# GpSimd's list per sequence in another order: the row scatter moved to the next step, the recurrence's double product moved ahead of a root

## The chip, the core and the metric

The program runs on one core of a Trainium2 chip. A core has five engines that run side by side, each through its own list in order: TensorE (PE; its weight loads are PEld), VectorE (DVE), ScalarE (ACT), GpSimd (POOL) and SyncE (SP), which here only issues DMAs. They meet through semaphores. The metric is device microseconds (us) of one execution, from three executions of each kernel.

## The reference, cut to what is computed

```python
# x, ctx: (32 sequences, 256 tokens, 256 channels), float32
x = ln(x + attn(x))          # attn: a complex decaying recurrence along the sequence axis
x = ln(x + xattn(x, ctx))    # 16 heads, 256x256 scores per head and sequence, softmax
x = ln(x + ffn(x))           # every token goes to one of 8 experts (nearest centroid)

# recurrence, written as a step over the 32 sequences: state = c * state + x[n]
# xattn: out = softmax(q k') v + q; out = ln_g * norm(out) + ln_b
# ffn: xn = rms_norm(x); id = argmin |xn - centroid|^2; h = xn @ up_w[id];
#      y = (a * silu(g)) @ down_w[id]; out = y + x
```

## The kernel before, in words

The kernel has two phases. Phase one walks over the 32 sequences ("items"), one per step `t`, software-pipelined: in step `t` TensorE makes the scores of item `t` and the transposed scores of `t-1`, the projections of item `n = t+1`, the output of item `a = t-2` and the expert choice of item `b = t-3`. At the end of its way each of an item's 256 rows (a token with its norm and its number) is written to its expert's bucket in DRAM, at a row number ("slot") worked out on the chip. Phase two takes tiles of 128 rows out of the buckets and runs the experts' matrices over them; the change does not touch it.

Each engine has a `step(t)` of its own, written out by hand; within it the order is fixed. VectorE's step is a chain of 16 row maxima of the scores (L1243, one per head `h`), with the other work put between the heads: at `h == 0` the normalised rows of item b (`row`, L1258, waits for `rstd2`, GpSimd's root for the second layer norm); at 3 `u = (state + 1) * x` (L1266); at 5 to 8 division, adding the queries (`oq`, L1370, twice) and the expert choice (`pick`, ending in `onehot`, L1405); at 9 the statistics `mvx` of the attention's norm; at 11 `gain` twice (L1377) with the small `place` (L1418) between; at 12 `slot` (L1425) and `y2` twice (L1324); at 13 and 14 the statistics of the second norm (`mv`, L1233, called mv2 below).

GpSimd's step, in order: `conv_products` of item t+3 (`by_re`, L694, one product of 128x1024 that serves both parts of the recurrence), `weigh(b)` (`xw`, L752), the bias added to x1 (L782), `cut` of the queries (`q_lo`, L770), `offset(b)` (L761), `conv_real` (L702), the root `rstd1` (L727, L729), `conv_imag` first half (L710), `cut` of the keys (`k_lo`, L770), `conv_imag` second half (L713), the root `rstdx` of the attention's norm (L727, L729), the scatter of item b (L802: two indirect DMAs of 128 rows, after a wait for VectorE's `slot`), `conv_input` (L720), the root `rstd2`, and the four small operations of `rms` (L738 to L744).

Around it: SyncE writes `k_lo` to DRAM when the cut is done and reads it back stacked (`k_st`), and the next step's scores on TensorE (L1004) wait for that. ScalarE squares `xw` for the expert choice (L927), which `offset` waits for. The `row` buffer and `slot` are double. Behind the last sequence `lower` (L1352) on VectorE prepares the experts' weights, a subtraction of 128x2048 each.

Of the kernel before, what the change touches and what calls it, by code (L numbers as in the profile page):

```python
# [15 lines left out]
SEQ, TOK, C = 32, 256, 256  # L16
NCH = C // P
NTC = TOK // P
# [9 lines left out]
PAD = E * CAP  # L28
# [4 lines left out]
SLOT = 6  # L33
# [48 lines left out]
def build(nc, x, ctx_in, lmlg, theta, last_conv, Wq, bq, Wk, bk, Wv, bv, ln_g, ln_b, ffn_scale, centroids, up_w, down_w, out):  # L82
    stack = ExitStack()
    with stack:
# [16 lines left out]
        buckets = nc.dram_tensor("buckets", (PAD + P, ROWW), F32)  # L101
# [19 lines left out]
        def sb1(name, shape, dt=F32):  # L121
            return phase1.enter_context(nc.sbuf_tensor(name, shape, dt))
# [69 lines left out]
        row = sb1("row", [P, 2, NTC, ROWW])  # L192
# [9 lines left out]
        slot = sb1("slot", [P, 2, NTC], U32)  # L202
# [25 lines left out]
        neg_in, scat = [s["neg_in0"], s["neg_in1"]], [s["scat0"], s["scat1"]]  # L228

        def wait(eng, name, item, per=1, j=None):  # L230

            if not item.runtime and item.k >= SEQ:
                item, j = Item(0, SEQ - 1), per
            wait_value(eng, name, item.times(per, per if j is None else j))

        def wait_value(eng, name, v):

            sm = s[name] if isinstance(name, str) else name
            if isinstance(v, int):
                if v > 0:  # L240
                    eng.wait_ge(sm, v)
            else:
                eng.wait_ge(sm, v)
                after_register_wait(eng)

        def wait_ring(eng, sm, item, ring, per):

            if not item.runtime:
                while item.k >= SEQ:
                    item = item - ring  # L250
            wait_value(eng, sm, item.uses(ring) * per)
# [6 lines left out]
        def steps(eng, body):  # L258

            for n in range(-2, SEQ + 3):  # L260
                body(Item(0, n))

        def active(item):
            return item.within(0, SEQ)
# [271 lines left out]
        with nc.Block() as block:  # L536
# [114 lines left out]
            def _(pool):  # L651
                g = nc.gpsimd
# [34 lines left out]
                def conv_products(item):  # L687

                    if not active(item):
                        return  # L690
                    wait(pool, "conv", item - 1, 5)
                    if item.k == 1:
                        wait(pool, "x1_ok", item - 1, 2)
                    g.tensor_tensor(by_re[:, :, :, :], state[:, 0].unsqueeze(1).to_broadcast(both), pair_b, ALU.mult).then_inc(s["conv"], 1)  # L694

                def conv_real(item):

                    if not active(item):
                        return
                    wait(pool, "conv", item, 5, 1)  # L700
                    wait(pool, "u_ok", item - 1)
                    g.tensor_tensor(state[:, 0], by_re[:, 1], state[:, 1], ALU.subtract).then_inc(s["conv"], 1)  # L702
# [12 lines left out]
                def conv_input(item):  # L715
                    if not active(item):
                        return
                    wait_ring(pool, x_in[item.mod(2)], item, 2, 16)
                    wait(pool, "conv", item, 5, 4)
                    g.tensor_tensor(state[:, 0], state[:, 0], xt[:, item.mod(2)], ALU.add).then_inc(s["conv"], 1)  # L720

                def rstd(item, ready, per, mv, rs, done):

                    if not active(item):
                        return
                    wait(pool, ready, item, per)
                    g.tensor_scalar(rs[:, 0], mv[:, :, 1], LN_EPS, None, ALU.add).then_inc(s[done], 1)  # L727
                    wait(pool, done, item, 2, 1)
                    g.tensor_tensor(rs[:, 1], rs[:, 0], neg_half[:, :].to_broadcast([P, NTC]), ALU.pow).then_inc(s[done], 1)  # L729

                def rms(item):

                    if not active(item):
                        return
                    p = item.mod(2)
                    wait(pool, "rstd2", item, 2)
                    wait_ring(pool, scat[p], item - 2, 2, 16 * NTC)
                    g.tensor_tensor(ms2[:, 0], mv2[:, :, 1], rs2[:, 1], ALU.mult).then_inc(s["rms"], 1)  # L738
                    wait(pool, "rms", item, 4, 1)
                    g.tensor_tensor(ms2[:, 1], ms2[:, 0], rs2[:, 1], ALU.mult).then_inc(s["rms"], 1)  # L740
                    wait(pool, "rms", item, 4, 2)
                    g.tensor_scalar(ms2[:, 2], ms2[:, 1], RMS_EPS, None, ALU.add).then_inc(s["rms"], 1)
                    wait(pool, "rms", item, 4, 3)
                    g.tensor_tensor(row[:, p, :, C], ms2[:, 2], neg_half[:, :].to_broadcast([P, NTC]), ALU.pow).then_inc(s["rms"], 1)  # L744

                def weigh(item):

                    if not active(item):
                        return
                    wait(pool, "x2_ok", item, 2)  # L750
                    wait(pool, "nx_ok", item - 1, 2)
                    g.tensor_tensor(xw[:, :, :], row[:, item.mod(2), :, 0:C], scale_bc[:, :].unsqueeze(1).to_broadcast([P, NTC, C]),  # L752
                                    ALU.mult).then_inc(s["xw_ok"], 1)

                def offset(item):

                    if not active(item):
                        return
                    wait(pool, "nx_ok", item, 2)
                    wait(pool, "pick", item - 1, PICK, 2)  # L760
                    g.tensor_tensor(dist[:, 0], cent_norm[:, :].unsqueeze(1).to_broadcast([P, NTC, E]),  # L761
                                    nx[:, :].unsqueeze(2).to_broadcast([P, NTC, E]), ALU.add).then_inc(s["offset"], 1)

                def cut(item, src, hi, lo, ready, done, out):

                    if not active(item):
                        return
                    wait(pool, ready, item, 4)
                    wait_ring(pool, out[(item - 1).mod(2)], item - 1, 2, 32)
                    g.tensor_tensor(lo[:, :, :], src, hi[:, :, :].bitcast(F32), ALU.subtract).then_inc(s[done], 1)  # L770

                def step(t):
                    n, a, b = t + 1, t - 2, t - 3
                    first = t.k < 0
                    if first:
                        rstd(t + 2, "ln1", 4, mv1, rs1, "rstd1")
                    conv_products(t + 3)
                    weigh(b)
                    if active(a):
                        wait(pool, "x1_ok", a, 2)  # L780
                        wait(pool, "x1T_pe", a)
                        g.tensor_tensor(x1[:, a.mod(4)], x1[:, a.mod(4)], b_bc[:, :].unsqueeze(1).to_broadcast([P, NTC, C]),  # L782
                                        ALU.add).then_inc(s["x1b_ok"], 1)
                    if n.k > 0:
                        cut(n, q32[:, :, :], q_hi, q_lo, "q_ok", "q_cut", q_out)
                    offset(b)
                    conv_real(t + 3)
                    if not first:
                        rstd(t + 2, "ln1", 4, mv1, rs1, "rstd1")
                    conv_imag(t + 3, 0)  # L790
                    if n.k > 0:
                        cut(n, k32[:, :, :], k_hi, k_lo, "k_ok", "k_cut", k_out)
                    conv_imag(t + 3, 1)
                    rstd(a, "lnx", 4, mvx, rsx, "rstdx")
                    if active(b):

                        p = b.mod(2)
                        wait(pool, "slot_ok", b, SLOT)
                        wait(pool, "id_ok", b)
                        wait(pool, "rms", b, 4)  # L800
                        for c in range(NTC):
                            g.indirect_dma_start(out=buckets[:, :], out_offset=bass.IndirectOffsetOnAxis(ap=slot[:, p, c:c + 1], axis=0),  # L802
                                                 in_=row[:, p, c, :], in_offset=None, bounds_check=PAD - 1,
                                                 oob_is_err=False).then_inc(scat[p], 16)
                    conv_input(t + 3)
                    rstd(a, "ln2", 4, mv2, rs2, "rstd2")
                    rms(a)

                steps(pool, step)
                gpsimd2(pool)  # L810

# [648 lines left out]
```

## Time and profile before

| what | us |
|---|---|
| three executions | 1263.86, 1266.94, 1254.69 (median 1263.86) |
| the profiled execution: its time | 1257.0 |
| its span, first to last instruction | 1255.2 |
| busy in it: PE, DVE, ACT, POOL | 1119.9, 942.7, 669.9, 783.9 |
| mean granted TensorE clock | 0.935 of full speed |

Busy shares are means over both phases. In phase one PE, DVE and POOL are all busy for most of a step, and in the second DVE and POOL wait for PE, so the change has to be read inside a step of phase one: what each engine does in order, and which wait ends last. All start times below are us from the span's start.

### The profile page before, as it was taken

Reading aid. Unit: us, or ns where it says so; the run is one execution under the profiler, and the core shown is the slowest. Engines: PE = TensorE matmul, PEld = TensorE weight load, DVE = VectorE, ACT = ScalarE, POOL = GpSimd, SP = SyncE. Lnnn points to the kernel's source line nnn. Section 1 sums busy time; section 2 is a strip of 40 time slices with the busy share of each in tenths; the row PEclk is TensorE's granted clock in tenths of the full one; section 3 lists DMA queues with packets and bytes.
Section 4 is the critical chain, followed back from the end, with each engine's and each line's share of the span. In section 5 each row is a group of like instructions: output and inputs, shape, how many; then the busy total and the mean of one; then the engine's idle time right before and its main releaser. Section 6 shows DMA issues by size and latency. Waiting matters only on the chain.

```text
span 1255.2 us, 27516 instructions
## 1 busy us (share of the span) xinstructions
PE 1119.9 (89%) x8060; PEld 820.0 (65%) x8061; DVE 942.7 (75%) x2416; ACT 669.9 (53%) x1416; POOL 783.9 (62%) x932
## 2 busy tenths in 40 slices
PE   3799989999999998989999999752999999999996
PEld 2466666666666666656666666431888888888885
DVE  7558998988988998999898898763555555555553
ACT  4166776766667776767676777641222222222221
POOL 4637888888878988879888865561233333333333
PEclk9689999999989999999999999555999999999998
DMA  4676676665555565556556555042111111111110
GB/s 131 146 179 194 174 207 183 182 156 139 141 140 146 149 158 137 147 139 161 136 146 156 136 134 126 11 151 59 44 51 47 43 50 50 49 47 48 50 51 22
DMA packets 90826, 144.91 MB, mean 115 GB/s; under 512 B 12663, under 2 KB 78336, under 8 KB 84513
## 3 DMA queue, kind: packets, MB, share of 16 engines
q1 hardware_dynamic: 83616, 126.09, 38.6%
q0 software_dynamic: 6528, 16.99, 4.6%
q8 instruction: 55, 0.90, 0.3%
q10 hardware_dynamic: 576, 0.53, 0.2%
q14 instruction: 51, 0.41, 0.1%
HBM read 91.44 MB, written 53.03 MB: 115 GB/s over the span
## 4 chain that ended last, share of the span: by engine, by line
PE 45%; DVE 19%; POOL 15%; issue 10%; DMA 8%; SPq 2%; ACT 1%; POOLq 0%; DVEq 0%; ACTq 0%
PE Y L454 10%; PE G L422 8%; PE A L422 8%; DVE neg_max_sb L1243 7%; PE S L1004 3%; PE M L988 3%; DMA k_st<-k_pieces 3%; DMA k_pieces<-k_lo 3%; DVE oq L1370 3%; POOL buckets L802 2%; PE GT L432 2%; PE O L980 2%; POOL rs L729 2%; POOL by_re L694 2%; PE M L960 2%
## 5 line engine op out<-in xcount | busy, mean ns | idle before, releaser
L1243 DVE TENSOR_REDUCE neg_max_sb<-S 128x2 f32<-128x512 f32 x512 | 328.3, 682 | 71.0 <-PE S L1004 69.2
L864 ACT ACTIVATE probs<-T 128x512 f32<-128x512 f32 x512 | 277.9, 595 | 148.1 <-PE T L1017 136.8
L1004 PE MATMUL S<-k_st,q_st 48*128 48x256 f32 x1024 | 215.3, 321 | 46.3 <-DMA k_st<-k_pieces 27.8
L1004 PEld LDWEIGHTS S<-k_st,q_st 48*128 48x128 f32 x1024 | 147.3, 194 | 123.7 <-issue 53.5
L1017 PE MATMUL T<-q_st,k_st 49*128 49x256 f32 x1024 | 211.9, 321 | 9.8 <-ACT probs L864 8.1
L1017 PEld LDWEIGHTS T<-q_st,k_st 49*128 49x128 f32 x1024 | 148.0, 195 | 28.3 <-ACT probs L864 17.0
L399 ACT ACTIVATE gT<-GT 128x512 f32<-128x512 f32 x71 | 42.5, 599 | 209.4 <-PE GT L432 209.4
L980 PE MATMUL O<-probs,v_aug 128*32 128x256 f32 x2048 | 151.0, 416 | 0.7 <-ACT probs L864 0.7
L378 POOL DMA_INDIRECT out<-res,token x71 | 76.4, 1077 | 103.3 <-DVE res L499 98.8
L454 PE MATMUL Y<-dn_sb,gT 128*128 x568 | 134.2, 379 | 0.8 <-ACT gT L399 0.8
L802 POOL DMA_INDIRECT buckets<-row,slot x64 | 69.7, 1089 | 85.0 <-DVE slot L1425 74.8
L454 PEld LDWEIGHTS Y<-dn_sb,gT 128*128 128x128 f32 x568 | 107.5, 189 | 18.3 <-issue 1.0
L422 PE MATMUL G<-up_hi,xsT 128*128 x284 | 107.7, 420 | 1.2 <-DVE xsT L504 1.0
L422 PE MATMUL A<-up_hi,xsT 128*128 x284 | 107.1, 418 | 0.0
L383 POOL TENSOR_SCALAR rs<-mv 128x1 f32<-128x1 f32 x71 | 16.0, 226 | 142.4 <-DVE mv L528 142.2
L499 DVE TENSOR_SCALAR res<-y,mv,rs 128x256 f32<-128x256 f32 x71 | 29.4, 414 | 86.1 <-POOL rs L385 86.1
L980 PEld LDWEIGHTS O<-probs,v_aug 128*32 128x32 f32 x2048 | 56.5, 115 | 56.2 <-ACT probs L864 16.0
L694 POOL TENSOR_TENSOR by_re<-state,decay 128x1024 f32<-128x1024 f32 x31 | 73.4, 2366 | 1.2 <-DVE x L1330 0.9
L403 ACT ACTIVATE gate<-G 128x512 f32<-128x512 f32 x71 | 42.4, 597 | 58.7 <-PE G L422 58.7
L988 PE MATMUL M<-ctT,wk_sb 128*128 128x256 f32 x256 | 67.0, 407 | 6.1 <-issue 6.0
L1116 PE MATMUL M<-wv_sb,ctT 128*128 128x256 f32 x256 | 70.5, 399 | 0.0
L988 PE MATMUL M<-x1T,wq_sb 128*128 128x256 f32 x256 | 68.2, 411 | 0.8 <-ACT x1T L877 0.8
(184 smaller groups left out, 2541.1 us busy)
## 6 DMA issues: line engine op xcount, KB each, us to landing
q_st<-q_pieces SPq DMA_DIRECT2D x64, 256.0 KB
k_st<-k_pieces SPq DMA_DIRECT2D x64, 256.0 KB
xr<-buckets SPq DMA_DIRECT2D x71, 129.0 KB, 2.1
xt<-in_x SPq DMA_DIRECT2D x32, 256.0 KB, 6.3
ct<-in_ctx SPq DMA_DIRECT2D x32, 256.0 KB, 6.8
q_pieces<-q_hi SPq DMA_DIRECT2D x32, 256.0 KB, 2.1
q_pieces<-q_lo SPq DMA_DIRECT2D x32, 256.0 KB, 2.2
q_st<-q_pieces SPq DMA_DIRECT2D x64, 128.0 KB
```

The lines of the kernel that those rows point to most:

```text
L378: g.indirect_dma_start(out=out_rows, out_offset=bass.IndirectOffsetOnAxis(ap=token[:, f.mod(2):f.mod(2) + 1], axis=0), in_=res[:, f.mod(2) ...
L422: last = t_.matmul(ps[:, :], xT[:, w, c * P:(c + 1) * P], src[:, bass.ds(off + c * 2 * HID, HID)], start=(k == 0), stop=(k == len(terms) - 1))
L454: last = t_.matmul(Y_ps[:, 0:C], gT[:, m.mod(2), c * P:(c + 1) * P], dn_sb[:, bass.ds(off + c * C, C)], start=(c == 0), stop=(c == HCH - 1))
L694: g.tensor_tensor(by_re[:, :, :, :], state[:, 0].unsqueeze(1).to_broadcast(both), pair_b, ALU.mult).then_inc(s["conv"], 1)
L802: g.indirect_dma_start(out=buckets[:, :], out_offset=bass.IndirectOffsetOnAxis(ap=slot[:, p, c:c + 1], axis=0), in_=row[:, p, c, :], in_of ...
L864: a_.activation(probs[:, h % 8].rearrange("p k t -> p (k t)"), T_ps[h % 2][:, :], ACT.Exp, scale=DH ** -0.5).then_inc(s["exp_ok"], 1)
L980: last = t_.matmul(O_ps[32 * j:32 * j + 32, (grp % 2) * TOK:(grp % 2 + 1) * TOK], v_aug[:, item.mod(4), kc, h * VW:h * VW + 32], probs[:, ...
L988: last = t_.matmul(dst[:, oc * TOK:(oc + 1) * TOK], w[:, ic, oc * P:(oc + 1) * P], xT[:, ic, :], start=(ic == 0), stop=(ic == NCH - 1))
L1004: last = t_.matmul(S_ps[h % 2][:, c * TOK:(c + 1) * TOK], q_st[base:base + STACK, h, c * P:(c + 1) * P], k_st[base:base + STACK, h, :], st ...
L1017: last = t_.matmul(T_ps[h % 2][:, c * TOK:(c + 1) * TOK], k_st[base:base + AUG, h, c * P:(c + 1) * P], q_st[base:base + AUG, h, :], start= ...
L1116: last = t_.matmul(M_ps[1][:, c * C:(c + 1) * C], ctT[:, ic, c * P:(c + 1) * P], wv_sb[:, ic, :], start=False, stop=(c == NTC - 1 and ic = ...
L1243: v.tensor_reduce(neg_max[:, cur.mod(2), :, h], S_ps[h % 2][:, :].rearrange("p (c t) -> p c t", c=NTC), AX.X, ALU.max, negate=True).then_i ...
```

## The change

Three things move in GpSimd's list; no instruction is added or taken away. The scatter of item b leaves its place behind `rstdx` and is issued one step later, behind `weigh` (for the last three items it stays in its own step, at the end). `conv_products` leaves the head of the step and is issued one step earlier, behind `conv_input` and ahead of `rstd2` (the first one stays at the head of the first step).

```diff
+                def scatter(item):
+                    if not active(item):
+                        return
+                    p = item.mod(2)
+                    wait(pool, "slot_ok", item, SLOT)
+                    wait(pool, "id_ok", item)
+                    wait(pool, "rms", item, 4)
+                    for c in range(NTC):
+                        g.indirect_dma_start(out=buckets[:, :], ...).then_inc(scat[p], 16)
...
-                    conv_products(t + 3)
                     weigh(b)
+                    if b.k - 1 < SEQ - 3:
+                        scatter(b - 1)
+                    if t.k == -2:
+                        conv_products(t + 3)
...
                     rstd(a, "lnx", 4, mvx, rsx, "rstdx")
-                    if active(b):
-                        p = b.mod(2)
-                        wait(pool, "slot_ok", b, SLOT)
-                        wait(pool, "id_ok", b)
-                        wait(pool, "rms", b, 4)
-                        for c in range(NTC):
-                            g.indirect_dma_start(out=buckets[:, :], ...).then_inc(scat[p], 16)
                     conv_input(t + 3)
+                    conv_products(t + 4)
                     rstd(a, "ln2", 4, mv2, rs2, "rstd2")
                     rms(a)
+                    if b.k >= SEQ - 3:
+                        scatter(b)
```

## Rows read from the trace of the kernel before

**Rows 1.** The page, busy us, share of the span and instructions per engine.

```profile
PE 1119.9 (89%) x8060; PEld 820.0 (65%) x8061; DVE 942.7 (75%) x2416; ACT 669.9 (53%) x1416; POOL 783.9 (62%) x932
```

**Rows 2.** One line's instructions, 136 to 733 us: count, ns minimum/median/maximum, first, last start.

```profile
L694 POOL TENSOR_TENSOR by_re<-state,decay x25: 2357/2369/2377, 138.4 to 710.8; 128x1024 f32<-128x1024 f32 x25
```

**Rows 3.** Windows of two steps: us, busy time (instructions) per engine, PEclk, DMA share, GB/s.

```profile
517.74:541.71 23.97, 21.64 (x196) 14.73 (x196) 23.08 (x56) 16.79 (x37) 19.82 (x23) 1.00 0.62 144
...
565.79:588.61 22.82, 21.35 (x197) 14.79 (x196) 21.80 (x59) 16.73 (x37) 20.32 (x23) 1.00 0.60 154
```

**Rows 4.** Waits, 136 to 733 us: who waited for whom, total us, times, longest.

```profile
POOL buckets L802 <- DVE slot L1425: 53.2, 25, 3.3
...
PE S L1004 <- DMA k_st<-k_pieces: 18.2, 12, 2.1
...
DVE row L1258 <- POOL rs L729: 11.1, 19, 0.8
```

**Rows 5.** Timeline of POOL: start us, us, engine, line, operation, out<-in, [idle before, releaser].

```profile
533.48 1.26 POOL L713 TENSOR_TENSOR state<-state,by_re 128x512 f32<-128x512 f32 x1
534.71 0.21 POOL L727 TENSOR_SCALAR rsx<-mvx 128x2 f32<-128x2 f32 x1
535.01 0.71 POOL L729 TENSOR_TENSOR rsx<-rsx,neg_half 128x2 f32<-128x2 f32 x1
538.97 1.08 POOL L802 DMA_INDIRECT buckets<-row,slot  x1 [3.26 <-DVE slot L1425]
...
541.36 1.30 POOL L720 TENSOR_TENSOR state<-state,xt 128x512 f32<-128x512 f32 x1
...
542.93 0.72 POOL L729 TENSOR_TENSOR rs<-rs,neg_half 128x2 f32<-128x2 f32 x1
...
545.29 2.37 POOL L694 TENSOR_TENSOR by_re<-state,decay 128x1024 f32<-128x1024 f32 x1
547.62 1.64 POOL L752 TENSOR_TENSOR xw<-row,scale_bc 128x512 f32<-128x512 f32 x1
```

**Rows 6.** Timeline of DVE in the same step.

```profile
532.27 1.28 DVE L1405 TENSOR_TENSOR onehot_bf<-expert_no,choice 128x16 bf16<-128x16 f32 x1
...
534.36 0.25 DVE L1233 BATCH_NORM_AGGREGATE mvx<-stx 128x2 f32<-128x6 f32 x2 [0.16 <-DVE stx L1227]
...
536.25 0.17 DVE L1418 TENSOR_TENSOR place<-place,onehot_bf 128x16 f32<-128x16 f32 x1
...
538.07 0.88 DVE L1324 SCALAR_TENSOR_TENSOR oq<-o,rsx,x 128x256 f32<-128x256 f32 x2
...
541.55 0.24 DVE L1233 BATCH_NORM_AGGREGATE mv<-st 128x2 f32<-128x6 f32 x2
...
545.68 2.53 DVE L1266 SCALAR_TENSOR_TENSOR u<-state,xt 128x512 f32<-128x512 f32 x1
```

**Rows 7.** Groups on DVE, 136 to 733 us; the first ends in busy us, mean ns, idle.

```profile
L1405 DVE TENSOR_TENSOR onehot_bf<-expert_no,choice 128x16 bf16<-128x16 f32 x25 | 13.1, 522 | 0.0
...
L1405 DVE TENSOR_TENSOR onehot_bf<-expert_no,choice x25: 155/188/1276, 149.1 to 723.4; 128x16 bf16<-128x16 f32 x25
...
L1266 DVE SCALAR_TENSOR_TENSOR u<-state,xt x25: 712/2515/2571, 138.8 to 713.6; 128x512 f32<-128x512 f32 x25
...
L1377 DVE SCALAR_TENSOR_TENSOR o<-oq,mvx,g_bc x50: 474/477/485, 152.6 to 726.4; 128x256 f32<-128x256 f32 x50
```

**Rows 8.** Timelines of DVE and POOL behind the last sequence's scores.

```profile
822.67 2.27 DVE L1352 TENSOR_TENSOR up_sb<-up_sb,up_hi 128x2048 fp32r<-128x2048 f32 x1
...
823.34 2.46 POOL L802 DMA_INDIRECT buckets<-row,slot  x1 [0.31 <-issue]
...
800.59 7.07 POOL L744 TENSOR_TENSOR row<-ms,neg_half 128x2 f32<-128x2 f32 x1
```

**Rows 9.** Timelines of SP (a DMA issue) and PE, one step.

```profile
484.67 0.38 SPq L572 DMA_DIRECT2D k_pieces<-k_lo  x1
...
493.35 0.50 PE L1004 MATMUL S<-k_st,q_st 48*128 48x256 f32 x2 [2.12 <-DMA k_st<-k_pieces]
```

More of the change, by code:

```diff
@@ L753, in weigh @@
                                     ALU.mult).then_inc(s["xw_ok"], 1)
+                def scatter(item):
[6 more added lines that the diff above has]
+                    for c in range(NTC):
+                        g.indirect_dma_start(out=buckets[:, :], out_offset=bass.IndirectOffsetOnAxis(ap=slot[:, p, c:c + 1], axis=0),
+                                             in_=row[:, p, c, :], in_offset=None, bounds_check=PAD - 1,
+                                             oob_is_err=False).then_inc(scat[p], 16)
                 def offset(item):
@@ L794, in step @@
                     rstd(a, "lnx", 4, mvx, rsx, "rstdx")
-                    if active(b):
-                        p = b.mod(2)
-                        wait(pool, "slot_ok", b, SLOT)
-                        wait(pool, "id_ok", b)
-                        wait(pool, "rms", b, 4)
-                        for c in range(NTC):
-                            g.indirect_dma_start(out=buckets[:, :], out_offset=bass.IndirectOffsetOnAxis(ap=slot[:, p, c:c + 1], axis=0),
-                                                 in_=row[:, p, c, :], in_offset=None, bounds_check=PAD - 1,
-                                                 oob_is_err=False).then_inc(scat[p], 16)
                     conv_input(t + 3)
+                    conv_products(t + 4)
                     rstd(a, "ln2", 4, mv2, rs2, "rstd2")
                     rms(a)
+                    if b.k >= SEQ - 3:
+                        scatter(b)
                 steps(pool, step)
```

## The prediction

> **What bounds the kernel now.** The page comes first: PE is busy for 89% of the span, DVE 75%, POOL 62% [rows 1]. That mixes two phases, and the change lies in the first, so one step of it is what to read. `by_re` runs once a step, 25 times from 138.4 to 710.8: (710.8 - 138.4) / 24 = 23.85 us a step [rows 2]. The windows show what fills a step: in the one of 23.97 us DVE is busy for 23.08, PE for 21.64, POOL for 19.82; another takes 22.82 with DVE at 21.80 [rows 3]. No engine is free enough to be ignored, and the order of their meetings decides. The waits tell which: POOL stands 53.2 / 25 = 2.1 us a step at the scatter, waiting for VectorE's `slot`; VectorE then stands 11.1 / 25 = 0.44 us for the root `rstd2`, which is queued behind that scatter; TensorE loses 18.2 / 25 = 0.73 us waiting for `k_st` [rows 4].
>
> Now the two timelines side by side, zero being 517.74, where the step of 23.97 us begins. POOL ends `conv_imag` at 17.0 and `rstdx` at 18.0, stands still until 21.2, issues the scatter until 23.6 and then does `conv_input` (1.30) and `rstd2`, whose root ends at 543.65, 1.94 into the next step [rows 5]. VectorE ends `mvx` at 16.9 and, with `gain`, `place`, `gain`, `slot`, `y2` between the maxima, ends mv2 at 541.79, 7.18 later [rows 6].
>
> What the reader should see next is how these two engines meet. `u` is issued 0.39 us after `by_re` started and ends 0.55 us after it ended: 2.53 us for an operation that takes 0.71 when alone [rows 5, 6, 7]. `onehot` takes 0.19 in the median and 1.28 when it stands behind `k_lo` [rows 6, 7]. So a VectorE operation with two inputs in SBUF waits out a large GpSimd operation, and the other way round. Yet `gain`, which also has two, takes 474 to 485 ns in all its 50 runs [rows 7], and `y2` is as steady in the step shown [rows 6]: they run between 18.0 and 21.2, where POOL stands still. The wait for `slot` looks like waste, but it keeps POOL off while VectorE does `gain`, `place` and `y2`.
>
> **The change part by part.** *The scatter leaves its place.* The wait (2.1 us mean) goes, and 2.4 us from the scatter's start to `conv_input` [rows 5]. What comes next there is `conv_input`, and behind it now `by_re`: 1.30 + 2.37 = 3.7 us of large operations, from about 18.0 to 21.7. `rstd2` then finds POOL idle and waits for mv2 instead; nothing else is queued behind it on POOL that VectorE needs earlier.
>
> *rstd2 earlier.* It now starts at mv2, so its root ends about 1.05 into the step (the small addition and the 0.72 us root [rows 5]) and not at 1.94. VectorE comes for it after two maxima, at about 1.3, so the wait of 0.44 us a step [rows 4] goes.
>
> *The head of the step.* `by_re` goes (2.37), the scatter comes (2.4). Walk: `rms` ends at 2.7 (1.05 plus the 1.6 between root and `by_re` in [rows 5]), `xw` runs to 3.9. `u` arrives at 3.3, waits 0.6 and ends at 4.6: it saves 1.3 us of DVE time. Does the scatter wait for `u`? Behind the loop one half of a scatter took 2.46 us beside a 2.27 us subtraction [rows 8] against 1.08 [rows 5], so I take that it does: 4.6 to 7.0. Before, `xw` ended at 549.26, 7.55 into the step [rows 5]; the bias add thus starts 0.5 earlier, and some 0.3 of that goes to the start of the scatter (in the step shown it starts 0.9 after `y2`, which itself follows `slot` [rows 5, 6], so a lead-in exists; bounds 0 to 0.9). All that follows to `conv_imag` is unchanged, and `oq` and `onehot` are squeezed between POOL's operations as before. So `conv_imag` still ends at 16.5 to 17.0, I take 17.0, the key cut stays within 0.5 us of its place, and `mvx` stays at 16.9. The DVE time saved at `u` is lost again waiting for POOL's `offset`, `oq` and `onehot`.
>
> On that scatter the Trainium skill ("SBUF — State Buffer", "Who interferes with whom") says that a two-input tensor operation takes only the read side of the port shared with GpSimd and infers that descriptor generation wants the write side; by it the scatter would not wait for `u`. The 2.46 us of [rows 8] speak against it; by the page the head would be 0.6 us a step shorter and the sum about 15 us lower.
>
> *The tail of the step, where it is decided.* Steps come in two kinds. A: `onehot` lost its race against a pending GpSimd operation and `mvx` is at 16.9. The mean of 522 ns between 0.17 and 1.28 [rows 7] gives (522 - 170) / 1110 = 0.32 of the steps. B: it won and `mvx` is 1.1 earlier, at 15.8. The same pair of engines will meet again, so I use 0.32 lost and 0.68 won for every race of two waiting operations.
>
> A: `conv_input` runs 18.0 to 19.3. The first `gain` arrives after two maxima, at 18.1. If it comes second it runs 19.3 to 19.75; `place`, not queued directly behind it, meets `by_re` (19.75 to 22.1) and waits. It began at 18.5 before, so the step loses 3.6. If `gain` comes first, `place` waits for `conv_input` (1.3), and `y2` later for the rest of `by_re` (1.1): 2.4. Half and half: 3.0, and 24.05 + 3.0 = 27.1.
>
> B: before, such a step took 22.8 [rows 3]. `gain` and `place` now fall beside the small operations of `rstdx` and lose 0.5; the first `y2` arrives at 19.7 while `conv_input` runs to 20.3, loses 0.6. Then `by_re` and the second `y2` race. Won, the step is 22.9 + 1.1 = 24.0; lost, 2.37 more, 26.4. Mean 0.68 x 24.0 + 0.32 x 26.4 = 24.8.
>
> Together 0.32 x 27.1 + 0.68 x 24.8 = 25.5, against 23.85: +1.7 us a step.
>
> *Transfers.* The scatter's two DMAs go out some 7 us into the step and not at 21 to 24; SP's queue is not touched, and `row` and `slot` are double, so nobody waits for them. `k_st` is issued from the same `k_lo` within 0.5 us: in the step shown from 484.67 to 493.35, 8.7 us, to the scores' start [rows 9]. In longer steps it arrives in time, so the 0.73 us of [rows 4] may go. I leave it out of the sum, since the B steps at 24.0 are no longer than k_st's arrival (15.8 + 8.7 = 24.5 at the worst).
>
> *Ends of the loop.* In the last three steps the scatter stands behind `rms`: `rstd2` comes up to 2.5 us earlier and `weigh` as much later. There `rms` and the scatter also stand behind the weight subtractions (7.07 us for one small root [rows 8]). Taken as 0, bounds -3 to +3.
>
> **Sum.** 25 steps x 1.7 = 42.5, rounded with the first and last step to +43: 1257.0 + 43 = 1300 us, in the profiled execution's own terms; the median of the runs shown is 7 us above it, 1.1% of spread lies among them, and I do not correct for it. Every step at 24.0 gives 25 x 0.15 = +4, 1261; every step at 27.1 gives 25 x 3.25 = +81, 1338.
>
> **The rivals.** *Same.* One wait takes the place of another (mv2 for `slot`), and the races at `y2` are won: all steps near 24.0, 1261 us. For it: `onehot` wins two of three; the mean margin is one `by_re` in every third or fourth step. Against it: A steps lose in either order.
>
> *Faster.* VectorE gets ahead of POOL: if the head is a full microsecond longer on POOL than I walk it, or `mvx` comes 2 us earlier, both `gain` and both `y2` are through before `conv_input` starts, and what is left is the saving at `u` and `rstd2`. Then all steps are like the short one, 22.8: 25 x -1.05 = -26, 1231 us. It decides from `conv_imag` ending more than 2.5 us behind `mvx`; in the step shown it is 0.1 [rows 5, 6]. Against it too: steps under 23 us meet the late `k_st` [rows 4].
>
> *Worst.* Each step loses as in A, 1338 us.
>
> By the same section of the Trainium skill the lock holds for a whole instruction and the loser blocks fully. No row here shows `gain`, `place` or `y2` blocked; `u` and `onehot` show it for their like.
>
> **How the numbers follow.** Slower by the mechanism 0.60, of which the worst 0.07; same 0.22; faster 0.18. The predicted time is 1300; the range leaves out most of the faster end and the tip of the worst: 1240 to 1338, the likeliest case's own being 1277 to 1335. One per cent, 12.6 us, is about what a measurement of this kernel can tell from no change: faster 0.18, same 0.22, slower 0.60.
>
> **What would show it.** Right: `gain`, `place` and `y2` with maxima of 1 to 2.5 us where they had 0.48; `u` below 1.5 in the median; POOL's wait at the scatter gone and one for mv2 (L727) of 2 to 4 us a step in its place; `conv_imag` unmoved against the step's start; steps of 24 and 26 to 27 us. Wrong: `gain` and `y2` still at 0.48 beside a running `by_re`, or `conv_input` starting after `y2`, or steps under 23 us.

## The result, and the profile after

The changed kernel takes 1372.66 us in the median of four executions (1353.0 to 1374.32), the kernel before 1265.4 beside it; the ratio is 1.0819, with a 95% interval of 1.0708 to 1.0929. (Executions fall in a faster or a slower state; the ratio is of the means of the faster ones, without the 1374.32 and with a fifth, of 1368.61.) It is slower, by more than the worst case of the forecast. The profiled execution took 1353.0 us, 96 more than the 1257.0 of the one before, and the sums below are made against that pair.

First the page's busy line of the kernel after, which answers to [rows 1], and the double product, which answers to [rows 2].

```profile
PE 1163.4 (86%) x8029; PEld 847.1 (63%) x8061; DVE 995.7 (74%) x2416; ACT 673.3 (50%) x1416; POOL 779.9 (58%) x932
```

```profile
L694 POOL TENSOR_TENSOR by_re<-state,decay x25: 2414/2567/2588, 138.1 to 793.0; 128x1024 f32<-128x1024 f32 x25
```

The product runs 25 times over 654.9 us, where it was 572.4. No engine has more instructions, but VectorE is busy for 53 us more and TensorE for 43.

Next one window over the 25 steps 4 to 28 (start of the first row maximum of step 4 to that of step 29), for before and then after; the columns are those of [rows 3].

```profile
134.72:731.84 597.12, 553.96 (x4853) 378.58 (x4854) 542.72 (x1403) 419.14 (x925) 506.26 (x551) 0.97 0.60 155
```

```profile
144.02:825.13 681.11, 595.83 (x4828) 404.18 (x4851) 591.35 (x1401) 423.17 (x925) 501.55 (x549) 0.88 0.54 135
```

Per step that is 23.88 us before and 27.24 after: 3.36 x 25 = 84 of the 96 us. Another 9 us lie ahead of it (step 4 begins at 144.0 where it was 134.7; 8 of them in the third and fourth step of the loop, which already run in the new order), and 3 behind it. VectorE's busy time per step went from 21.71 to 23.65 us, +1.94; its idle time from 2.17 to 3.59, +1.42. The granted clock of TensorE fell from 0.97 to 0.88.

The waits of after in the loop, 136 to 820 us, answer to [rows 4]:

```profile
POOL rs L727 <- DVE mv L1242: 96.4, 25, 5.5
PE S L1013 <- DVE neg_max_sb L1252: 81.8, 39, 3.3
DVE neg_max_sb L1252 <- PE S L1013: 81.3, 59, 2.6
```

The same two waits of TensorE and VectorE in the kernel before, 136 to 733 us:

```profile
DVE neg_max_sb L1243 <- PE S L1004: 34.1, 28, 2.5
...
PE S L1004 <- DVE neg_max_sb L1243: 13.3, 20, 1.1
```

GpSimd's wait for `slot` has gone, and 96.4 / 25 = 3.9 us a step for mv2 stand in its place. The other two are new in size: TensorE waits 81.8 / 25 = 3.3 us a step for VectorE's maxima, where it waited 0.5, and VectorE waits 3.3 us for scores, where it waited 34.1 / 25 = 1.4.

Groups on DVE in the same stretch, which answer to [rows 7] (busy us, mean ns, idle), and `u` from 136 to 830 us (ns minimum/median/maximum); behind them `y2` of the kernel before, 136 to 733 us:

```profile
L1333 DVE SCALAR_TENSOR_TENSOR oq<-o,rsx,x 128x256 f32<-128x256 f32 x50 | 59.9, 1237 | 0.0
L1386 DVE SCALAR_TENSOR_TENSOR o<-oq,mvx,g_bc 128x256 f32<-128x256 f32 x51 | 31.2, 611 | 0.0
L1427 DVE TENSOR_TENSOR place<-place,onehot_bf 128x16 f32<-128x16 f32 x25 | 18.8, 753 | 0.0
L1434 DVE CAST slot<-slot_f 128x2 uint32<-128x2 f32 x25 | 12.7, 507 | 0.0
L1339 DVE TENSOR_SCALAR x<-u,mv,rs 128x256 f32<-128x256 f32 x50 | 18.4, 410 | 2.7
L1267 DVE TENSOR_SCALAR row<-oq,mv,rs 128x256 f32<-128x256 f32 x50 | 18.3, 408 | 0.0
```

```profile
L1275 DVE SCALAR_TENSOR_TENSOR u<-state,xt x26: 679/1516/2526, 149.8 to 829.1; 128x512 f32<-128x512 f32 x26
```

```profile
L1324 DVE SCALAR_TENSOR_TENSOR oq<-o,rsx,x 128x256 f32<-128x256 f32 x50 | 21.9, 480 | 0.0
```

`y2` (L1333) was at 480 ns, `gain` (L1386) at 477, `place` (L1427) at 169 and the cast to `slot` (L1434) at 160 on average. `x1` (L1339, the first layer norm's result, behind `y2`) is still at 410. `row` (L1267) no longer waits for `rstd2`.

The timelines show two kinds of step. VectorE in the end of the step that began at 526.56 (kind B), with `u` of the next step as the last line, and GpSimd beside it:

```profile
547.61 1.28 DVE L1252 TENSOR_REDUCE neg_max_sb<-S 128x2 f32<-128x512 f32 x2
548.80 0.65 DVE L1434 CAST slot<-slot_f 128x2 uint32<-128x2 f32 x1
549.36 2.99 DVE L1333 SCALAR_TENSOR_TENSOR oq<-o,rsx,x 128x256 f32<-128x256 f32 x2
...
560.66 0.74 DVE L1275 SCALAR_TENSOR_TENSOR u<-state,xt 128x512 f32<-128x512 f32 x1
```

```profile
548.15 1.27 POOL L720 TENSOR_TENSOR state<-state,xt 128x512 f32<-128x512 f32 x1
549.50 2.57 POOL L694 TENSOR_TENSOR by_re<-state,decay 128x1024 f32<-128x1024 f32 x1
555.29 0.22 POOL L727 TENSOR_SCALAR rs<-mv 128x2 f32<-128x2 f32 x1 [3.22 <-DVE mv L1242]
```

The cast stands until `conv_input` ends at 549.42. The first `y2` runs in its 0.47 us, from 549.36 to 549.83; `by_re`, issued meanwhile at 549.50, takes its turn as soon as it ends, and the second `y2` stands behind it until 552.07: the pair takes 2.99 us where it took 0.88 [rows 6]. In the next step, from 555.12, the other kind (A):

```profile
570.37 1.26 DVE L1414 TENSOR_TENSOR onehot_bf<-expert_no,choice 128x16 bf16<-128x16 f32 x1
...
573.87 1.45 DVE L1386 SCALAR_TENSOR_TENSOR o<-oq,mvx,g_bc 128x256 f32<-128x256 f32 x1
...
575.32 2.25 DVE L1427 TENSOR_TENSOR place<-place,onehot_bf 128x16 f32<-128x16 f32 x1
```

Here the first `gain` stands behind `conv_input` (1.45 us) and the tiny `place` behind `by_re`. Of the 25 steps, told apart by what is blocked, 7 are of kind A (28.3 us on average), 17 of kind B (27.0), and the last, which has no double product in its tail, takes 24.1.

What follows on TensorE, in windows of 2 us through the end of that B step and the head of the A step:

```profile
549.00:551.00 2.00, 2.00 (x28) 1.46 (x20) 2.00 (x3) 1.13 (x3) 1.92 (x2) 1.00 0.93 180
551.00:553.00 2.00, 0.26 (x3) 0.01 (x1) 1.89 (x3) 1.14 (x3) 1.07 (x1) 1.00 0.98 156
553.00:555.00 2.00, 0.40 (x4) 0.42 (x4) 2.00 (x6) 0.00 (x0) 0.00 (x0) 1.00 1.22 188
555.00:557.00 2.00, 2.00 (x17) 1.25 (x18) 2.00 (x8) 1.46 (x3) 1.38 (x5) 0.66 0.67 124
557.00:559.00 2.00, 2.00 (x19) 0.73 (x20) 0.21 (x2) 0.48 (x2) 1.92 (x3) 0.50 0.79 216
559.00:561.00 2.00, 2.00 (x15) 1.71 (x16) 1.54 (x3) 1.50 (x3) 1.53 (x3) 0.98 0.05 19
```

and TensorE's own timeline there:

```profile
548.49 1.07 PE L989 MATMUL O<-probs,v_aug 128*32 128x256 f32 x16
...
554.60 0.35 PE L1013 MATMUL S<-k_st,q_st 48*128 48x256 f32 x1 [3.34 <-DVE neg_max_sb L1252]
...
556.95 1.94 PE L989 MATMUL O<-probs,v_aug 128*32 128x256 f32 x16
```

With VectorE held up, no buffer of scores comes free, and TensorE stands for 3.3 us, to 554.6. (So it does in every step B; in A the gap is 2.2 us.) Then the granted clock is 0.66 and 0.50 for four microseconds, 0.50 being the lower of the two levels (1.2 GHz), though the engine is busy throughout. The same product of probabilities takes 121 ns a piece (1.94 / 16) where it took 67 (1.07 / 16). Over the 25 steps a mean of 0.88 means the lower level for about 0.24 of the time, some 160 us; the 0.97 before means some 36. The scores of the next step's head come late, VectorE waits for them, and the step loses time where GpSimd holds nobody up.

### The profile page after: what moved, and what is told of

It reads as the page before. It is cut to its first block, busy times and chain, and to the rows that moved or that the text cites. A ratio compares the mean times of both kernels' runs of the same rounds, so it can differ in the third digit from the quotient of the medians.

```text
span 1351.2 us, 27485 instructions
## 1 busy us (share of the span) xinstructions
PE 1163.4 (86%) x8029; PEld 847.1 (63%) x8061; DVE 995.7 (74%) x2416; ACT 673.3 (50%) x1416; POOL 779.9 (58%) x932
## 4 chain that ended last, share of the span: by engine, by line
PE 53%; DVE 34%; issue 6%; DMA 3%; POOL 2%; SPq 1%; ACT 1%; POOLq 0%; DVEq 0%; ACTq 0%
DVE neg_max_sb L1252 11%; PE Y L454 9%; PE G L422 8%; PE A L422 7%; PE S L1013 7%; PE M L997 5%; DVE oq L1333 5%; PE O L989 5%; DVE oq L1379 3%; PE M L969 3%; PE GT L432 2%; PE M L1078 2%; DVE o L1386 2%; DVE st L1236 2%; DVE x L1339 2%
## 5 line engine op out<-in xcount | busy, mean ns | idle before, releaser
L1013 PE MATMUL S<-k_st,q_st 48*128 48x256 f32 x1024 | 228.6, 340 | 103.3 <-DVE neg_max_sb L1252 89.8
L1013 PEld LDWEIGHTS S<-k_st,q_st 48*128 48x128 f32 x1024 | 160.3, 210 | 188.3 <-issue 129.3
L1026 PE MATMUL T<-q_st,k_st 49*128 49x256 f32 x1024 | 225.9, 339 | 8.0 <-ACT probs L873 6.8
L1026 PEld LDWEIGHTS T<-q_st,k_st 49*128 49x128 f32 x1024 | 159.7, 211 | 24.3 <-ACT probs L873 15.7
L989 PE MATMUL O<-probs,v_aug 128*32 128x256 f32 x2048 | 165.8, 450 | 0.7 <-ACT probs L873 0.7
L378 POOL DMA_INDIRECT out<-res,token x71 | 76.5, 1077 | 103.3 <-DVE res L499 98.8
L454 PEld LDWEIGHTS Y<-dn_sb,gT 128*128 128x128 f32 x568 | 107.5, 189 | 18.2 <-issue 1.0
L989 PEld LDWEIGHTS O<-probs,v_aug 128*32 128x32 f32 x2048 | 59.7, 122 | 64.7 <-issue 27.2
L727 POOL TENSOR_SCALAR rs<-mv 128x2 f32<-128x2 f32 x64 | 16.1, 251 | 143.8 <-DVE mv L1242 132.4
L499 DVE TENSOR_SCALAR res<-y,mv,rs 128x256 f32<-128x256 f32 x71 | 29.4, 414 | 86.1 <-POOL rs L385 86.1
L694 POOL TENSOR_TENSOR by_re<-state,decay 128x1024 f32<-128x1024 f32 x31 | 77.9, 2513 | 3.3 <-DVE x L1339 0.9
L997 PE MATMUL M<-x1T,wq_sb 128*128 128x256 f32 x256 | 77.1, 451 | 0.8 <-ACT x1T L886 0.8
L783 POOL TENSOR_TENSOR q_lo<-q,q_hi 128x512 fp32r<-128x512 f32 x31 | 39.5, 1274 | 58.5 <-ACT q L909 58.4
```

The costliest lines, as they stand in the source:

```text
L378: g.indirect_dma_start(out=out_rows, out_offset=bass.IndirectOffsetOnAxis(ap=token[:, f.mod(2):f.mod(2) + 1], axis=0), in_=res[:, f.mod(2) ...
L454: last = t_.matmul(Y_ps[:, 0:C], gT[:, m.mod(2), c * P:(c + 1) * P], dn_sb[:, bass.ds(off + c * C, C)], start=(c == 0), stop=(c == HCH - 1))
L989: last = t_.matmul(O_ps[32 * j:32 * j + 32, (grp % 2) * TOK:(grp % 2 + 1) * TOK], v_aug[:, item.mod(4), kc, h * VW:h * VW + 32], probs[:, ...
L997: last = t_.matmul(dst[:, oc * TOK:(oc + 1) * TOK], w[:, ic, oc * P:(oc + 1) * P], xT[:, ic, :], start=(ic == 0), stop=(ic == NCH - 1))
L1013: last = t_.matmul(S_ps[h % 2][:, c * TOK:(c + 1) * TOK], q_st[base:base + STACK, h, c * P:(c + 1) * P], k_st[base:base + STACK, h, :], st ...
L1026: last = t_.matmul(T_ps[h % 2][:, c * TOK:(c + 1) * TOK], k_st[base:base + AUG, h, c * P:(c + 1) * P], q_st[base:base + AUG, h, :], start= ...
```

## The experiments

Three theories were to be told apart. *Lock* (in the first texts: port): large GpSimd operations now run under VectorE's tail and hold it up. *Head*: the scatter at the step's head pushes what follows it there, whatever the tail does. *Clock*: what the gap on TensorE does to its granted clock costs time of its own.

| kernel | ratio to before, 95% interval | us a step (4 to 28) | clock there |
|---|---|---|---|
| before | 1 | 23.88 | 0.97 |
| the change | 1.0819 [1.0708, 1.0929] | 27.24 | 0.88 |
| e1 scatter alone | 1.0585 [1.0518, 1.0652] | 26.48 | 0.91 |
| e2 product alone | 1.0303 [1.0238, 1.0369] | 25.33 | 0.97 |
| e3 change, wait for y2 | 1.0842 [1.0747, 1.0937] | 27.96 | 0.90 |
| e4 change, TensorE kept busy | 1.0615 [1.0543, 1.0687] | 26.28 | 0.98 |
| e5 change, wait for y2 and x1 | 1.0246 [1.0198, 1.0294] | 24.98 | 0.97 |
| e6 before, conv_input ahead of rstdx | 1.0123 [1.0076, 1.0171] | 24.52 | 0.94 |
| e7 before, product behind weigh | 1.0070 [1.0037, 1.0104] | 24.20 | 0.97 |
| e8 e1 with e5's wait | 1.0429 [1.0381, 1.0476] | 25.87 | 0.92 |
| e9 change, product in halves | 1.0752 [1.0678, 1.0826] | 27.36 | 0.88 |
| e11 before, TensorE kept busy | 1.0195 [1.0133, 1.0257] | 24.77 | 0.98 |

One per cent is 12.6 us. The kernel before ran beside each of them, at 1255 to 1265 us.

**The two halves of the change (e1, e2).** The scatter moved alone, the product staying at the head; and the product moved alone, the scatter staying where it was.

```diff
  e1, against the change
+                    conv_products(t + 3)
                     weigh(b)
                     if b.k - 1 < SEQ - 3:
                         scatter(b - 1)
...
-                    conv_products(t + 4)
  e2, against the kernel before
-                    conv_products(t + 3)
+                    if t.k == -2:
+                        conv_products(t + 3)
...
                     conv_input(t + 3)
+                    conv_products(t + 4)
                     rstd(a, "ln2", 4, mv2, rs2, "rstd2")
```

> The scatter alone is moved to the next step; by_re stays at the head of the step. Port theory (what costs is that conv_input and by_re run where VectorE does gain, place, slot and y2): y2 falls back from 1.24 to 0.48 us in the mean, since no by_re is near it; gain or slot still lose up to 1.3 to conv_input; the head of POOL's step is longer by the scatter less the earlier rstd2, some 1.5 us, so the key cut is later. Steps of 24 to 25 us, 1262 to 1290. Head theory (what costs is the scatter's 2.4 us ahead of the two cuts, so that k_st and TensorE are late): most of the loss stays, 1320 or more, with TensorE waiting for k_st.

> by_re alone is moved, behind conv_input and ahead of rstd2; the scatter stays in its place with its wait for slot. Port theory: gain, place, slot and y2 all run as when alone (0.48, 0.17, 0.16, 0.48), because POOL stands still for slot and then issues the scatter; by_re delays rstd2 by 2.4 us, so VectorE waits some 2.8 us for it at row, and gets back some 1.3 us at u: steps of 24.5 to 25.5, 1272 to 1300. Head theory: the head is 2.4 us shorter and the scatter is not in it, so no loss against the kernel before, 1240 to 1265.

Measured: +5.9% and +3.0%. In e1 (DVE groups and a wait, 136 to 733 us):

```profile
L1384 DVE SCALAR_TENSOR_TENSOR o<-oq,mvx,g_bc 128x256 f32<-128x256 f32 x44 | 38.6, 876 | 0.0
L1412 DVE TENSOR_TENSOR onehot_bf<-expert_no,choice 128x16 bf16<-128x16 f32 x22 | 23.2, 1052 | 0.0
...
DVE dist L1395 <- POOL dist L774: 29.4, 18, 2.3
```

`gain` meets `conv_input`, which no wait for `slot` holds back now. The head, with scatter and product both in it, is later, so that VectorE waits for `offset` (29.4 us in some 22 steps) and `onehot` meets `k_lo` in most steps (1052 ns on average, 522 before). So the time is the one that the head theory gave, but not by its cause: TensorE waits for `k_st` only 4.2 us in the whole stretch, and `y2` is back at 473 ns, as the other theory had it. In e2 the wait for `slot` still covers the tail; `gain`, `place` and `y2` are at 477, 168 and 478 ns, and the loss is one wait:

```profile
DVE row L1260 <- POOL rs L729: 74.7, 24, 3.3
```

3.1 us a step, because the double product now lies between mv2 and `rstd2`. Either half alone costs time, and in part for other reasons than both together.

**The tail (e3, e5, e9).** GpSimd waits until `y2` is done (e3), or until `x1` is done too (e5), before it begins `conv_input` and the product; and the product is cut into two operations of half its length (e9).

```diff
  e3
+                    if active(a):
+                        wait(pool, "y_ok", a, 4)
                     conv_input(t + 3)
  e5
+                    if active(t + 2):
+                        wait(pool, "x1_ok", t + 2, 2)
                     conv_input(t + 3)
  e9
-                    g.tensor_tensor(by_re[:, :, :, :], state[:, 0]..., pair_b, ALU.mult)
+                    g.tensor_tensor(by_re[:, 0], state[:, 0], im_b, ALU.mult)
+                    g.tensor_tensor(by_re[:, 1], state[:, 0], re_b, ALU.mult)
```

> The changed kernel with one wait more: GpSimd waits for both y2 before conv_input. No work is added. Port theory: the four operations run as when alone, TensorE's gap of 3.3 us goes, and with it the lower clock; by_re ends some 0.9 us behind mv2, so row waits as in the kernel before: steps of 23.5 to 24.5, 1245 to 1280, although GpSimd idles more. Head theory: the scatter is still at the head, so 1330 or more. If the whole loss were the lock, but the clock had a cause of its own, y2 is short and the granted clock stays near 0.88: about 1310.

Measured: +8.4%, as bad as the change itself, though the four operations were back at their old times. The loss had moved one place on. The DVE group (136 to 733 us), then one such pair and GpSimd beside it:

```profile
L1341 DVE TENSOR_SCALAR x<-u,mv,rs 128x256 f32<-128x256 f32 x44 | 83.9, 1947 | 2.4
...
559.99 3.82 DVE L1341 TENSOR_SCALAR x<-u,mv,rs 128x256 f32<-128x256 f32 x2
...
559.96 1.28 POOL L720 TENSOR_TENSOR state<-state,xt 128x512 f32<-128x512 f32 x1 [1.65 <-DVE oq L1335]
561.32 2.34 POOL L694 TENSOR_TENSOR by_re<-state,decay 128x1024 f32<-128x1024 f32 x1
```

The first half of `x1` waits for `conv_input` and the second for `by_re`: 3.82 us for a pair that takes 0.73 in the changed kernel. It has one tensor input (and scalars), so the class named in the prediction, operations with two inputs in SBUF, was too narrow. The Trainium skill ("SBUF — State Buffer", "Who interferes with whom") counts `cast` and `tensor_scalar` among the operations that can take the shared ports, and the 0.65 us of the cast and the 1.95 of `x1` agree with it.

> The changed kernel, with GpSimd waiting for VectorE's whole epilogue of step t+2 (gain, place, cast to slot, y2, both halves of x1) before it begins conv_input and the double product. No VectorE operation of the tail can then meet them. Lock theory (the tail's collisions, now with the cast and x1 counted in, and the lower clock that follows from the gap that they leave on TensorE, are most of the loss): gain, place, the cast, y2 and x1 all at the times they have alone (0.17 to 0.5 us), the second root is now late instead and the row waits 2 to 3.5 us for it as in the run with the product alone; steps of 25 to 25.8 us, granted clock of the loop above 0.95, 1285 to 1305 us. Head theory (the scatter at the head is most of it, whatever the tail does): not under 1325.

Measured: +2.5%, 1288.72 us in the median, as the lock theory had it. Waits and groups, 136 to 733 us:

```profile
POOL state L720 <- DVE x L1341: 98.1, 24, 4.2
...
DVE row L1269 <- POOL rs L729: 33.1, 23, 1.7
...
DVE dist L1399 <- POOL dist L774: 25.5, 22, 1.3
...
L1335 DVE SCALAR_TENSOR_TENSOR oq<-o,rsx,x 128x256 f32<-128x256 f32 x48 | 21.0, 478 | 0.0
```

GpSimd now stands 4.1 us a step and the kernel is 5.3% faster than the change (1.0246 / 1.0819): about 72 of its 103 us come from what meets in the tail, the lower clock behind it included, and what the added wait itself costs taken off. (The 103 is 8.19% of 1256 us.) What is left is `row` waiting for the root (1.4 us a step) and VectorE waiting for `offset` (1.1).

> The changed kernel with the double product written as two operations of half its length (128x512 each in place of 128x1024), the same work in all. If a VectorE operation that meets a GpSimd operation waits to the end of that one instruction, the second y2 waits for half as long: 2.6 us becomes about 1.4, TensorE's gap behind it is 1.2 us shorter, and the steps are about 1 us shorter: 1310 to 1340 us. If VectorE only shares the port with the whole of the product, or waits until GpSimd is idle, nothing changes: 1350 to 1375. If each half takes the place again ahead of the waiting VectorE operation, y2 stays at 2.6 as well.

Measured: +7.5%, the same as the change within the intervals. VectorE and GpSimd in one tail:

```profile
554.89 1.90 DVE L1335 SCALAR_TENSOR_TENSOR oq<-o,rsx,x 128x256 f32<-128x256 f32 x2
556.90 1.49 DVE L1341 TENSOR_SCALAR x<-u,mv,rs 128x256 f32<-128x256 f32 x2
...
555.03 1.48 POOL L695 TENSOR_TENSOR by_re<-state,decay 128x512 f32<-128x512 f32 x1
556.48 1.45 POOL L696 TENSOR_TENSOR by_re<-state,decay 128x512 f32<-128x512 f32 x1
```

The second `y2` is released by the end of the first half, so a VectorE operation does wait to the end of one GpSimd instruction; it took 1.5 us and not 2.6. But the second half then takes its turn ahead of `x1`: 1.49 us for that pair. The time was only spread over two operations. My expectation of 1310 to 1340 had reckoned with a half coming next at the second `y2`, but not with the half that comes next at `x1`.

**The head (e8).** e1 with the wait of e5 ahead of `conv_input`, so that nothing meets in the tail.

```diff
  against e1
+                    if active(t + 2):
+                        wait(pool, "x1_ok", t + 2, 2)
                     conv_input(t + 3)
```

> The scatter at the head of the next step and the double product behind it at the head too (as in the run with the scatter alone), and conv_input held until VectorE's epilogue of step t+2 is over. What is left against the kernel before is the head's order alone: scatter, then the product. Lock theory: gain, place and y2 at their own times; the head 1.5 to 2 us later than before (onehot blocked by the product about 1 us, u by what follows), steps of 25 to 25.7 us, 1285 to 1305 us. If the scatter at the head costs all of the run with the scatter alone: 1320 to 1335.

Measured: +4.3%, between the two expectations. `gain` and `y2` are at their old times, and the crowded head costs 2 us a step (25.87 against 23.88): VectorE waits for `offset` (41.9 us in 23 steps) and `onehot` is blocked most of the time.

```profile
DVE dist L1397 <- POOL dist L774: 41.9, 19, 2.3
...
L1414 DVE TENSOR_TENSOR onehot_bf<-expert_no,choice 128x16 bf16<-128x16 f32 x23 | 25.4, 1105 | 0.0
```

So in e1 the collision of `gain` with `conv_input` is about 0.6 us a step (26.48 - 25.87), and the crowded head, with scatter and double product both in it, is the rest. What the scatter alone costs in the head of the changed kernel no run shows; in e5 it is in the 1.1 us a step that are left (24.98 - 23.88), together with the late root.

**The clock (e4, e11).** 24 transposes of a constant at the end of TensorE's steps 3 to 27, into a spare buffer that nobody reads: in the changed kernel (e4) and in the kernel before (e11).

```diff
+                            if 3 <= t.k <= 27:
+                                wait(pe, "v_ok", n)
+                                for k in range(24):
+                                    t_.transpose(M_ps[1][...], ident[:, :], ident[:, :])
```

> The changed kernel with 24 transposes more on TensorE at the end of steps 3 to 27, behind the context's transposes, whose result nothing reads: they fill 2.6 us of the gap of 3.3 us that the blocked y2 leaves. Clock theory (about half of the loss is TensorE's lower granted clock behind that gap): y2 and place as long as before, the granted clock in the loop from 0.88 to 0.95 or more, VectorE's wait for the scores from 81 us to some 40, and 20 to 40 us less than the changed kernel: 1315 to 1335, in spite of the added work. If the clock costs nothing: the same 1353 to 1373, or some us more.

> The kernel before with the same 24 transposes of a constant at the end of steps 3 to 27, their results unread, as in the run on the changed kernel: what the transposes cost or give by themselves. Their time there was about 1 us a step. If the 40 us that they gave the changed kernel came from a clock that the tail's gap had lowered (0.883 in its loop, 0.971 in the loop of the kernel before), they give nothing here: granted clock of the loop 0.98, 1245 to 1275 us. If they help any kernel of this shape as much: 1215 to 1230.

Measured: added work makes the changed kernel 2% faster (1.0819 to 1.0615, 26 us; the intervals do not overlap) and the kernel before 2% slower (24 us). Each ratio is to the kernel before beside it; the 40 us in the expectation of e11 compare medians of different sittings. Loop windows of e4 and e11:

```profile
144.77:801.76 656.99, 608.10 (x5404) 440.83 (x5428) 584.12 (x1402) 421.74 (x925) 501.63 (x549) 0.98 0.56 140
```

```profile
133.28:752.45 619.17, 605.02 (x5428) 436.71 (x5424) 556.13 (x1401) 417.30 (x925) 497.93 (x549) 0.98 0.57 149
```

In e4 the collisions are all still there (`y2` at 1077 ns on average, `place` at 1076), the clock is 0.98, and the step is 1 us shorter. By e11 the transposes give nothing of themselves. VectorE's wait for scores fell from 81 to 64 us in the 25 steps, not to the 40 that I expected. The meetings also fell otherwise: the gain lies in the steps B (24.7 us on average for 27.0), while A stays at 28.3 and comes 11 times for 7, and `u` takes 0.68 us in every step. So the runs do not part what the clock gives from what the changed meetings give or take. If the transposes are free in e4, since they lie in the gap, the lowered clock, with the meetings that it moves, costs the changed kernel 26 us; if they cost there what they cost in e11, some 50. Two runs do not fix it closer. My 1245 to 1275 for e11 was short by 4 us.

**Two orders meant to beat the kernel before (e6, e7).** With the kernel before as the base: `conv_input` ahead of `rstdx`; and, apart from that, the double product behind `weigh`.

```diff
  e6
+                    conv_input(t + 3)
                     rstd(a, "lnx", 4, mvx, rsx, "rstdx")
  ...
-                    conv_input(t + 3)
                     rstd(a, "ln2", 4, mv2, rs2, "rstd2")
  e7
-                    conv_products(t + 3)
                     weigh(b)
+                    conv_products(t + 3)
```

> The kernel before with one thing moved: conv_input of step t+3 from behind the second root's subtraction to a place ahead of it, so that by_re, still at the head, begins about 0.9 us earlier than it did; the scatter stays where it was. Theory of the order (what costs is a long GpSimd product under two-input VectorE work; conv_input there is short and meets the maxima's wait): the 0.4 us that the row waits for the second root go or stay, by_re ends about 0.9 us earlier, u about 0.5 us shorter; 0.4 to 0.9 us a step, 1235 to 1248 us. Rival: conv_input meets gain and place as it did in the changed kernel, and pushes the tail by up to 1 us: 1255 to 1285.

> The kernel before with one thing moved within the head: the double product by_re from ahead of weigh (xw) to behind it. u then meets xw alone, and not by_re and xw in turn (the shortest u at 0.66 us, 2.0 on average in the kernel before). If the lock in the head is part of what a step costs there: u 1.0 to 1.5 us, xw and with it the routing's norm 2 us earlier, 0.3 to 0.8 us a step, 1235 to 1248 us. If u's wait is hidden (VectorE stands for TensorE's scores just behind it anyway) or by_re now meets onehot or another operation instead: 1250 to 1262. If by_re pushes the bias of x1 and q_lo later, and these set the head: 1265 to 1290.

Measured: +1.2% and +0.7%, both slightly slower, with intervals that leave out 1; I had hoped for 1235 to 1248. (The expectation of e6 names the old place wrongly: `conv_input` stood behind the scatter and ahead of `rstd2`.) In e6 the rival came true, with `place` as the victim (136 to 733 us):

```profile
L1418 DVE TENSOR_TENSOR place<-place,onehot_bf 128x16 f32<-128x16 f32 x24 | 23.2, 969 | 0.0
```

In e7 `u` fell from 2.0 to 1.44 us, but `onehot` rose from 0.52 to 0.77, VectorE waited longer for scores (38.6 us for 34.1) and 7.9 us for `offset`: the gain at `u` was given back within the same step. No order that I ran beats the kernel before.

## Why the prediction was wrong, point by point

*What bounds the kernel, and the cover.* Right, and it is what the change stands on: the wait for `slot` [rows 4] kept GpSimd off `gain`, `place` and `y2`. e2 keeps that wait and they stay at 477, 168 and 478 ns; the change drops it and they do not; e5 puts a wait back and they do. The class of operations was too narrow: the cast (0.16 us on average before, 0.51 after) and, in e3, `x1` belong to it.

*rstd2 earlier.* Right: `row` waits for nothing (idle 0.0, where VectorE stood 0.44 us a step). The 0.44 us is less than the wait for scores that now stands right behind `row` (2.25 us before 559.46, in the step shown).

*The head.* Half right. `u` fell from 2.00 to 1.55 us on average (median 1.52, so not under the 1.5 named). But it came at 5.6 us into the step on average (560.66 - 555.12 = 5.5 in the step shown), not at 3.3: the scores were late. In 13 of the 25 steps it was issued while the scatter's second half ran, and lost to that and to the bias addition behind it, 2.3 to 2.5 us in all. In the other 12 it went through beside the scatter (0.68 to 0.75 us), whose second half took longer in 6 of them only (1.17 to 1.49 us for 0.97); the walk has the scatter wait for `u` every time. And `conv_imag` was not unmoved: `rstdx` begins 17.7 us into the step shown (572.80 - 555.12), where it was 17.0, and 18.2 on average over the 25 steps, where it was 17.4.

*The tail: the step that failed.* It is "0.32 lost and 0.68 won for every race". In B the race of the second `y2` with `by_re` was lost 17 times of 17 (2.58 to 2.61 us each time). It is no race: `by_re` is issued while the first `y2` runs and is next in turn when that ends. In A `gain` came second 7 times of 7, where the walk had it half and half. The share from `onehot` came from another meeting and could not be carried over. The two kinds of step did come, with `gain`, `place` and `y2` as the blocked ones, and 7 of 24 were A, against 0.32. With every such race lost the prediction's own walk gives A 24.05 + 3.6 = 27.65, B 26.4, and (7 x 27.65 + 17 x 26.4 + 24) / 25 = 26.65 us a step and not 25.5: 29 us more.

*The base of the walk.* It started too low. The two kinds stand on steps of 24.05 and 22.8 us, which with the same shares make 0.32 x 24.05 + 0.68 x 22.8 = 23.2; the result was then compared with the mean of 23.85. That hides 0.65 us a step, 16 us. In the trace of the kernel before, the 17 steps in which `onehot` wins take 23.7 us on average and not 22.8 (the other 8 take 24.25): in 8 of the 17 VectorE waits 2.6 to 4.7 us for scores. The 22.82 of [rows 3] is one of the shortest.

*What is missing.* No term of the sum followed the blocked `y2` to TensorE. It empties TensorE for 3.3 us; the granted clock falls to the lower level for the head of the next step; and VectorE's wait for scores rises by 1.9 us a step, less the 0.44 that `row` no longer waits. In turn the walk's tail was too dear. Against its own base it lengthens a step by 26.65 - 23.2 = 3.45 us, nearly all of it VectorE held up; measured are 3.36, but only 1.94 of them are VectorE's busy time and 1.42 its waiting. In B the cast loses 0.5 us and the second `y2` 2.1, while the 0.5 at `gain` and `place` and the 0.6 at the first `y2` did not come. That the two errors cancel is luck.

*Ends of the loop.* Taken as 0 within 3 either way; they were 12: 9 ahead of step 4, 8 of these because two more steps run in the new order than the 25 I counted, and 3 behind step 28.

*The sum.* Forecast +43; lost races 29, the base 16, the ends 12: 100 against the measured 96, with the missing wait and the dear tail cancelling.

*Transfers.* Right: `k_st`'s wait of 0.73 us a step is gone (none is left between 136 and 820 us), and the scatter's DMAs, now early in the step, kept nobody waiting.

*The rivals.* The worst, every step losing as in A (1338), was the nearest; I gave it 0.07, since I read the races as independent. Same and faster both needed steps that get through their tail beside the product; none but the last, which has none there, did.

## What to carry to other kernels

A wait that looks like waste on one engine can be the cover for another engine's work on a shared port: before removing it, list every operation that runs inside it, on the other engine, and cost each at the length of the instruction that will move in. A meeting of two instructions was decided here, 17 times of 17, by who was already pending, so a share of won races seen at one place is no probability at another; walk it to the start times. Check that the kinds of step on which a walk stands make up the mean from which it is to differ. Follow a stall to TensorE's next idle stretch too: here a 3 us gap was paid a second time, at least in part in the clock of the work behind it.

## What the runs showed of the hardware

- In the rows shown a VectorE operation with two inputs in SBUF that meets a running GpSimd tensor operation waits to the end of that one instruction, whatever its own size: `place` of 0.17 us took 2.25, and with the product in halves `y2` took 1.5 and not 2.6.
- Operations with one tensor input are held up too: the cast of 128x2 (0.65 us for 0.16) and the `tensor_scalar` of 128x256 (1.95 us on average for 0.41). The row maxima, whose input is the scores in PSUM, are not: a pair takes 1.28 us while `conv_input` runs beside it (547.61 to 548.89 above).
- The indirect DMA's issue on GpSimd is in it in part: in e5 its first half took 1.34 us where it met `u`, against 1.09 alone. In the changed kernel, e3 and e9 `u` got through (0.68 to 0.75 us) in all 30 steps in which it was issued at most 0.30 us behind the start of the second half, and lost (2.24 to 2.53 us) in all 45 in which it was issued 0.31 us or more behind it. What the issue holds, and when, stays open. The Trainium skill ("SBUF — State Buffer", "Who interferes with whom") infers that a `tensor_tensor` would not block it; the 1.34 us beside `u`, a `scalar_tensor_tensor` with two inputs, and the 2.46 us beside a `tensor_tensor` in [rows 8] are against that.
